# Attention maxima taken one bank at a time, exponentials taken two banks at a time

## The chip, the cores and the metric

The kernel runs on one core of one Trainium2 chip. The metric is the device time of one execution in microseconds (us); the median of three timed runs of the kernel before is 1527.36 us (1527.1 to 1528.5). Of the core's engines this case concerns TensorE (PE, matrix products, and PEld, its weight loads), VectorE (DVE), ScalarE (ACT), GpSimd (POOL) and SyncE (SP, which issues DMAs). TensorE's clock has two levels, 1.2 and 2.4 GHz; a granted clock of 0.50 is the lower one and 1.00 the higher.

## The reference

Two layers follow one another on 4096 tokens of width 128: attention, a mixture of experts, a selective state-space block and a second mixture of experts. Only the attention is touched:

```python
x = L0_attn_x                                   # 4 x 1024 x 128
x = x + _L0_attn_ref(_layernorm(x), wq, w_down, wk_up, wv_up, wo)
...
def _L0_attn_ref(x, wq, w_down, wk_up, wv_up, wo):      # H = 16 heads, D = 8
    q = (x @ wq).reshape(B, T, H, D)
    lat = x @ w_down
    k, v = (lat @ wk_up).reshape(B, T, H, D), (lat @ wv_up).reshape(B, T, H, D)
    q, k = _apply_rope(q, cos, sin), _apply_rope(k, cos, sin)
    scores = jnp.einsum('bqhd,bkhd->bhqk', q, k) * scale
    allowed = pages[None, :] <= pages[:, None]          # pages of 32 tokens
    scores = jnp.where(allowed, scores, finfo.min)
    attn = jax.nn.softmax(scores, axis=-1)
    return jnp.einsum('bhqk,bkhd->bqhd', attn, v).reshape(B, T, E) @ wo
```

## The kernel before

The kernel is a row of blocks, one after another, each with its own instruction list for every engine and semaphores between them. The block concerned is `attend` (from L496). There are 64 pairs of batch and head; they are done in NG = 16 groups of four heads. In a group a "pair" is two heads whose rows lie in partitions 0 to 63 (r = 0) and 64 to 127 (r = 1), so that two matmuls of different r work on different rows of the array.

For every group the work has three strands.

- Maxima. The query-by-key scores are computed once only to find each query's largest score. The allowed blocks of a pair are cut into NK = 9 items of 512 columns, so a group has NI = 18 items. For an item m, `maxima(m)` (L679) writes two PSUM banks, r = 0 and r = 1; `take(m)` (L612) reduces both on VectorE in one instruction over 2 x 512 elements. The item banks are 0 to 3, two per item, so item m needs the banks of item m-2. After the 18th item `combine` (L623) makes the row maxima, GpSimd negates and splits them in bf16 parts, TensorE transposes these (`turn`, L695), ScalarE copies the result to `neg_rows` (`turned`, L644), and SyncE writes them by DMA into rows of the query operand.
- Scores. `scores(i, k, pair)` (L700) computes the key-by-query scores again, now less the maximum, for k = 0 to 8 and two pairs: again two banks of 512 columns. ScalarE exponentiates them, one instruction for each bank (L666), into `prob` in SBUF. The score banks are 4 to 6, used one after another in a ring of three.
- Values. `values(i, v)` (L717) multiplies the values with `prob`, 18 pieces of 256 columns for a group, and accumulates in bank 7. ScalarE copies bank 7 out once a group (`store`, L651).

What sets the order is the loop of the TensorE list (L735 to L756). A lead of LEAD = 26 items of maxima comes first. Then a group has 18 turns, numbered here 0 to 17 (turn = 2k + pair). A turn issues the maxima of one item 26 ahead, the scores of its own k and pair, and the value pieces that are due (L473: one piece in most turns, none in turn 3, two in turn 12). At the end of turn 14 TensorE does the transposition for the next group. All engines take their lists in order, so whatever waits holds up all that stands behind it. The waits around the change are: `maxima(m)` on `max_taken` (L685), `scores` on `exp_done` (L705), in turn 15 also on `neg_stored` (L707), the values of turn 4 on `out_stored` (L726), `take` on `max_scores_done` (L614). ScalarE's `store` of the group before stands between the exponentials of k = 1, pair 1 (L668), and `turned` after the first exponential of k = 7 (L670).

Of the kernel before, what the change touches and what calls it, by code (L numbers as in the profile page):

```python
# [15 lines left out]
P = 128  # L16
# [11 lines left out]
GH = 4  # L28
# [423 lines left out]
]  # L452
NC = 4
MAX_BANK, SCORE_BANK, VALUE_BANK = 0, 4, 7
SCORE_RING = 3
PROB_RING = 4
TURN_K = 7
PIECE = 256
# [37 lines left out]
def attend(nc, g):  # L496

    with ExitStack() as ctx:
# [19 lines left out]
        out_written = [sem(f"out_written{k}") for k in range(2)]  # L518
        block = ctx.enter_context(nc.Block())
        NEG_STEPS = 5  # L520
        UNITS = GH * NK

        def neg_bank(i):

            unit = UNITS * i + GH * TURN_K + 2
            return PS[0:2 * 3 * GP * NJ, SCORE_BANK + unit % SCORE_RING, 0:P // 2].bitcast(BF16)

        def rows(t, count, i, pair, r, first, n):
            return t[HROWS * r:HROWS * r + count, i % RING, pair, first:first + n]

        @block.sync
        def _(sp):
            def store(i):
                sp.wait_ge(out_stored, i + 1)
                sp.dma_start(g.heads[GH * i:GH * (i + 1), :, :, :].rearrange("h k r t -> (h k r) t"), out_sb[:, i % 2, :]).then_inc(out_written[i % 2], 16)

            def neg_in_rows(i):
                sp.wait_ge(neg_stored, i + 1)
                for r in range(2):
                    at, rows_of = HROWS * r + ROWS_QK, 3 * GP * NJ  # L540
                    sp.dma_start(qr[at:at + 3, i % RING, :, :].rearrange("r p t -> r (p t)"),
                                 neg_rows[rows_of * r:rows_of * (r + 1), :]).then_inc(neg_in, 16)

            for n in range(ROWS_BEGUN, RING * ROW_DMAS):
                load_rows(sp, g, n // ROW_DMAS, n % ROW_DMAS)
                if n == 2 * ROW_DMAS - 1:
                    neg_in_rows(0)
            for i in range(NG):
                if i >= 1 and i + RING - 1 < NG:
                    sp.wait_ge(scores_done, UNITS * i)  # L550
                    for n in range(ROW_DMAS):
                        load_rows(sp, g, i + RING - 1, n)
                if i >= 1:
                    store(i - 1)
                if i == NG - 1:

                    for k in range(2):
                        sp.wait_ge(out_written[k], 16 * (EARLY // GH // 2))
                    sp.dma_start(sums[:, :], g.heads[0:EARLY, :, D, :]).then_inc(sums_in, 16)
                    sp.wait_ge(inverted, 1)  # L560
                    sp.dma_start(g.inverses[0:EARLY, :, :].rearrange("i a (k t) -> i (a k) t", k=CPB), sums[:, :]).then_inc(inverse_out, 16)
                else:
                    neg_in_rows(i + 1)
            store(NG - 1)
            for k in range(2):
                sp.wait_ge(out_written[k], 16 * NG // 2)
            sp.wait_ge(inverse_out, 16)
# [39 lines left out]
        @block.vector  # L607
        def _(dve):
            dve.memset(found[:, :, :, :], -3e38).then_inc(bottom_set, 1)
            dve.wait_ge(bottom_set, 1)  # L610

            def take(m):  # L612

                dve.wait_ge(max_scores_done, m + 1)  # L614
                pair, item = divmod(m % NI, NK)
                _, n, first, step = MAXIMA[item]
                bank = MAX_BANK + 2 * (m % 2)
                dve.tensor_reduce(found[:, :, pair, first:first + (n - 1) * step + 1:step],  # L618
                                  PS[:, bank:bank + 2, :].rearrange("p r (w n) -> p r w n", w=n), AX.X, ALU.max).then_inc(max_taken, 1)
                if m % NI == NI - 1:  # L620
                    combine(m // NI)

            def combine(i):  # L623

                dve.wait_ge(max_taken, NI * (i + 1))
                if i > 0:
                    dve.wait_ge(neg_steps, NEG_STEPS * (i - 1) + 1)
                even, odd = (row_max[:, :, :, k::2].rearrange("p r q j -> p (r q) j") for k in range(2))
                every = found[:, :, :, :].rearrange("p r q (j c) -> p (r q) j c", c=NC)
                dve.tensor_reduce(even, every[:, :, 0:NJ // 2, :], AX.X, ALU.max)  # L630
                dve.tensor_reduce(odd, every[:, :, NJ // 2:NJ, :], AX.X, ALU.max).then_inc(row_max_ready, 1)

            for m in range(NG * NI):
                if m % NI == 0 and m > 0:
                    dve.wait_ge(row_max_ready, m // NI)
                take(m)
            dve.wait_ge(sums_in, 16)
            dve.reciprocal(sums[:, :], sums[:, :]).then_inc(inverted, 1)

        @block.scalar  # L640
        def _(act):
            act.preload_act_table(ACT.Exp)

            def turned(i):  # L644

                act.wait_ge(neg_turned, 1 + i + 1)
                if i > 0:
                    act.wait_ge(neg_in, 32 * i)
                act.activation(neg_rows[:, :], neg_bank(max(i - 1, 0)), ACT.Copy).then_inc(neg_stored, 1)

            def store(i):  # L651
                act.wait_ge(values_done, NV * (i + 1))
                if i >= 2:
                    act.wait_ge(out_written[i % 2], 16 * (i // 2))
                act.activation(out_sb[:, i % 2, :], PS[:, VALUE_BANK, :], ACT.Copy).then_inc(out_stored, 1)  # L655

            turned(0)
            for i in range(NG):
                for k in range(NK):
                    step = NK * i + k  # L660
                    if step >= PROB_RING:
                        act.wait_ge(values_done, NV // NK * (step - PROB_RING + 1))
                    for h in range(GH):
                        unit = UNITS * i + GH * k + h
                        act.wait_ge(scores_done, unit + 1)
                        act.activation(prob[:, step % PROB_RING * GH + h, :], PS[:, SCORE_BANK + unit % SCORE_RING, :], ACT.Exp,  # L666
                                       scale=float(D) ** -0.5).then_inc(exp_done, 1)
                        if k == 1 and h == 2 and i > 0:  # L668
                            store(i - 1)
                        if k == TURN_K and h == 0 and i < NG - 1:  # L670
                            turned(i + 1)
            store(NG - 1)

        @block.tensor
        def _(pe):
# [3 lines left out]
            def maxima(m):  # L679

                i, (pair, item) = m // NI, divmod(m % NI, NK)
                if m % NI == 0:
                    pe.wait_ge(rows_in[i % RING], ROW_LOADS * (i // RING + 1))
                if m >= 2:
                    pe.wait_ge(max_taken, m - 1)  # L685
                at = 0
                for q_block, key, n, diagonal in MAXIMA[item][0]:
                    count = ROWS_D if diagonal else ROWS_QK
                    for r in range(2):
                        last = pe.matmul(PS[:, MAX_BANK + 2 * (m % 2) + r, at:at + n], rows(qr, count, i, pair, r, q_block * P, P),  # L690
                                         rows(kr, count, i, pair, r, key, n), start=True, stop=True)
                    at += n
                last.then_inc(max_scores_done, 1)

            def turn(i):  # L695

# [1 line left out]
                pe.transpose(neg_bank(max(i - 1, 0)), neg_parts[:, :, :, :].rearrange("p r s n -> p (r s n)"), g.identb[:, :]).then_inc(neg_turned, 1)  # L698

            def scores(i, k, pair):  # L700
                unit = UNITS * i + GH * k + 2 * pair
                if k == 0 and pair == 0:
                    pe.wait_ge(neg_in, 32 * (i + 1))
                if unit >= 2:
                    pe.wait_ge(exp_done, unit - 1)  # L705
                if k == TURN_K and pair == 1 and i < NG - 1:
                    pe.wait_ge(neg_stored, i + 2)  # L707
                last = {}
                for col, j, q, w, diagonal in KEYS[k]:
                    count = ROWS_D if diagonal else ROWS_M  # L710
                    for r in range(2):
                        last[r] = pe.matmul(PS[:, SCORE_BANK + (unit + r) % SCORE_RING, col:col + w], rows(kr, count, i, pair, r, j * P, P),  # L712
                                            rows(qr, count, i, pair, r, q, w), start=True, stop=True)
                for r in range(2):
                    last[r].then_inc(scores_done, 1)

            def values(i, v):  # L717

                k = v // (NV // NK)
                step = NK * i + k  # L720
                if v % (NV // NK) == 0:
                    pe.wait_ge(exp_done, UNITS * i + GH * (k + 1))
                if v == 0:
                    pe.wait_ge(v1_ready, CPB * (i + 1))
                    if i > 0:
# [13 lines left out]
            for i in range(NG):  # L739
                for k in range(NK):  # L740
                    for pair in range(GP):
# [7 lines left out]
                        for v in DUE[GP * k + pair]:  # L749
                            values(i, v)  # L750
                        if k == TURN_K and pair == 0 and i < NG - 1:
                            pe.wait_ge(exp_done, UNITS * i + GH * TURN_K)
                            turn(i + 1)
            for v in range(NV):
                if due(v) >= 2 * NK:
# [1234 lines left out]
```

## Time and profile before

| | us |
|---|---|
| median of 3 runs | 1527.36 |
| the profiled execution | 1529.38 |
| its span, first to last instruction | 1527.6 |
| VectorE's maxima (L618), first and last start | 93.7 and 441.4 |
| last exponential (L666) starts | 472.2 |

The profile is of one execution. Its span is cut into windows, in which each engine's busy time can be compared with the window's length; the timeline prints single instructions, with runs of equal neighbours merged in one row (start, length of the whole run, engine, line, count). In square brackets stands how long the engine sat idle before, and what ended that. Matmul ends are modelled. On VectorE and ScalarE the record of an instruction overlaps the start of the next one, so the distance from start to start is shorter than the duration of one.

### The profile page before, as it was taken

Reading aid. Unit: us, or ns where it says so; the run is one execution under the profiler, and the core shown is the slowest. Engines: PE = TensorE matmul, PEld = TensorE weight load, DVE = VectorE, ACT = ScalarE, POOL = GpSimd, SP = SyncE. Lnnn points to the kernel's source line nnn. Section 1 sums busy time; section 2 is a strip of 40 time slices with the busy share of each in tenths; the row PEclk is TensorE's granted clock in tenths of the full one; section 3 lists DMA queues with packets and bytes.
Section 4 is the critical chain, followed back from the end, with each engine's and each line's share of the span. In section 5 each row is a group of like instructions: output and inputs, shape, how many; then the busy total and the mean of one; then the engine's idle time right before and its main releaser. Section 6 shows DMA issues by size and latency. Waiting matters only on the chain. (4 is left out here: it accounts for less than half of the span.)

```text
span 1527.6 us, 22335 instructions
## 1 busy us (share of the span) xinstructions
PE 1258.2 (82%) x7696; PEld 582.4 (38%) x7696; DVE 1130.1 (74%) x1298; ACT 720.4 (47%) x1121; POOL 576.3 (38%) x405
## 2 busy tenths in 40 slices
PE   4937999999995769999996676878867867877998
PEld 2412333433333734454443212322322322356565
DVE  5768999999953544444445879999999999964544
ACT  2515999999995133333333783323333323303221
POOL 2320110101002203222334058998989988921000
PEclk9957999999997569999996887998999998985999
DMA  3321111111104200000001004333333323300000
GB/s 101 122 86 48 55 60 45 54 53 59 38 17 113 85 0 0 1 0 0 0 0 28 2 12 145 126 118 107 124 124 124 124 104 108 119 21 9 14 15 27
DMA packets 50302, 91.19 MB, mean 60 GB/s; under 512 B 9495, under 2 KB 25511, under 8 KB 50215
## 3 DMA queue, kind: packets, MB, share of 16 engines
q1 hardware_dynamic: 49710, 89.66, 18.2%
q8 instruction: 54, 0.88, 0.2%
q10 hardware_dynamic: 504, 0.37, 0.1%
q14 instruction: 34, 0.27, 0.1%
HBM read 76.25 MB, written 13.37 MB: 59 GB/s over the span
## 5 line engine op out<-in xcount | busy, mean ns | idle before, releaser
L618 DVE TENSOR_REDUCE att_found<-PS 128x2 f32<-128x1024 f32 (+2 forms) x288 | 333.1, 1218 | 10.8 <-PE PS L690 8.9
L1515 PE MATMUL PS<-ms_ch,ident_sb 128*128 128x512 f32 x512 | 277.6, 670 | 70.3 <-POOL ms_ch L1622 70.3
L666 ACT ACTIVATE att_prob<-PS 128x512 f32<-128x512 f32 x576 | 313.4, 596 | 28.3 <-PE PS L712 15.3
L1622 POOL TENSOR_TENSOR ms_ch<-xnT,ms_c_rows 128x1024 f32<-128x1024 f32 x128 | 302.8, 2378 | 49.2 <-PE PS L1515 26.7
L1580 DVE TENSOR_TENSOR_SCAN xnT<-ms_decay,PS 128x1024 f32<-128x1024 f32 x96 | 216.0, 2275 | 4.5 <-DVE PS L1567 0.5
L731 PE MATMUL PS<-att_prob,att_v 128*32 128x256 f32 (+1 forms) x2560 | 181.8, 370 | 3.0 <-ACT att_out L655 2.8
L1515 PEld LDWEIGHTS PS<-ms_ch,ident_sb 128*128 128x128 f32 x512 | 100.2, 207 | 196.2 <-POOL ms_ch L1622 105.5
L1553 ACT ACTIVATE PS<-m_dt,m_a 128x1024 f32<-128x1024 f32 x32 | 35.8, 1118 | 265.4 <-DVE xnT L1580 265.4
L1027 POOL TENSOR_TENSOR f_yT<-f_yT,f_prod 128x512 f32<-128x512 f32 x56 | 71.0, 1268 | 209.0 <-DVE f_prod L1082 209.0
L690 PE MATMUL PS<-kr,qr 55*128 55x128 bf16 (+4 forms) x1152 | 120.8, 290 | 29.7 <-PEq L256 16.0
L712 PE MATMUL PS<-qr,kr 55*128 55x128 bf16 (+4 forms) x1152 | 114.0, 275 | 14.8 <-ACT att_prob L666 8.2
L1567 DVE TENSOR_TENSOR PS<-ms_dtu,PS 128x1024 f32<-128x1024 f32 x96 | 115.0, 1213 | 12.3 <-PE PS L1506 12.1
L1550 ACT ACTIVATE ms_decay<-m_dt,m_a 128x1024 f32<-128x1024 f32 x96 | 106.2, 1138 | 14.4 <-DVE xnT L1580 14.4
L1082 DVE SCALAR_TENSOR_TENSOR f_prod<-PS,e_w_b,f_x3s 128x512 f32<-128x512 f32 x56 | 42.0, 750 | 84.3 <-PE PS L1151 73.5
L1506 PE MATMUL PS<-m_bc,m_w_sel_b 96*128 96x512 bf16 x192 | 62.9, 413 | 34.9 <-DVE xnT L1580 25.2
L690 PEld LDWEIGHTS PS<-kr,qr 48*128 48x128 bf16 (+1 forms) x1152 | 39.6, 97 | 135.5 <-issue 92.6
L1042 ACT ACTIVATE f_h<-PS,e_w_b 128x512 f32<-128x512 f32 x64 | 44.0, 687 | 94.8 <-PE PS L1139 94.8
L731 PEld LDWEIGHTS PS<-att_prob,att_v 128*32 128x32 f32 x2560 | 54.7, 108 | 62.2 <-issue 53.5
L1629 POOL TENSOR_TENSOR ms_x_row<-ms_dtu,ms_b_row 128x1024 f32<-128x1024 f32 x32 | 75.1, 2346 | 1.3 <-DMA ms_b_row<-bc_rows_dram 1.3
L1580 DVE TENSOR_TENSOR_SCAN xnT<-PS,ms_x_row 128x1024 f32<-128x1024 f32 x32 | 72.5, 2266 | 0.0
L595 POOL COPY att_v<-V 128x256 f32<-128x256 f32 x32 | 11.8, 398 | 156.4 <-PE PS L731 156.1
L177 PE MATMUL PS<-ident_sb,norm_xn 128*128 128x128 f32 x128 | 35.1, 431 | 42.5 <-DVE norm_xn L164 42.0
(214 smaller groups left out, 1784.5 us busy)
## 6 DMA issues: line engine op xcount, KB each, us to landing
ms_c_rows<-bc_rows_dram SPq DMA_DIRECT2D x64, 512.0 KB, 5.6
ms_b_row<-bc_rows_dram SPq DMA_DIRECT2D x32, 512.0 KB, 3.8
qk_parts_dram<-qkv_parts SPq DMA_DIRECT2D x48, 128.0 KB, 1.8
heads_dram<-att_out SPq DMA_DIRECT2D x16, 256.0 KB, 2.4
qr<-qk_parts_dram SPq DMA_DIRECT2D x32, 96.0 KB
qr<-qk_parts_dram SPq DMA_DIRECT2D x96, 32.0 KB
kr<-qk_parts_dram SPq DMA_DIRECT2D x96, 32.0 KB
kr<-qk_parts_dram SPq DMA_DIRECT2D x32, 96.0 KB
```

What stands on the lines that cost most here:

```text
L618: dve.tensor_reduce(found[:, :, pair, first:first + (n - 1) * step + 1:step], PS[:, bank:bank + 2, :].rearrange("p r (w n) -> p r w n", w= ...
L666: act.activation(prob[:, step % PROB_RING * GH + h, :], PS[:, SCORE_BANK + unit % SCORE_RING, :], ACT.Exp, scale=float(D) ** -0.5).then_in ...
L690: last = pe.matmul(PS[:, MAX_BANK + 2 * (m % 2) + r, at:at + n], rows(qr, count, i, pair, r, q_block * P, P), rows(kr, count, i, pair, r, ...
L712: last[r] = pe.matmul(PS[:, SCORE_BANK + (unit + r) % SCORE_RING, col:col + w], rows(kr, count, i, pair, r, j * P, P), rows(qr, count, i, ...
L731: last = pe.matmul(PS[VW * h:VW * (h + 1), VALUE_BANK, q - half * CH:q - half * CH + w], v1[:, i % 2, half, h, j, :], prob[:, step % PROB_ ...
L1027: pool.tensor_tensor(yT[:, k, :], yT[:, k, :], prod[:, e % 2, :], ALU.add).then_inc(summed, 1)
L1515: last = pe.matmul(PS[:, Y_BANK + 2 * half + q, :], g.ident[:, :], ch[:, half, q * CH:(q + 1) * CH], start=j == 0 and not odd, stop=j == J ...
L1550: act.activation(decay[:, 2 * odd + half, :], m.dt[:, half, sequence(b)], ACT.Exp, scale=m.a[:, half, n + odd:n + odd + 1]).then_inc(decay ...
L1567: dve.tensor_tensor(inputs(half), dtu[:, half, :], inputs(half), ALU.mult).then_inc(input_ready, 1)
L1580: dve.tensor_tensor_scan(h[:, odd, half, :], factor, x, 0.0, ALU.mult, ALU.add).then_inc(scanned, 1)
L1622: pool.tensor_tensor(ch[:, half, :], h[:, odd, half, :], c_rows[:, s % C_RING, :], ALU.mult).then_inc(ch_ready, 1)
L1629: pool.tensor_tensor(x_row[:, :], dtu[:, 1, :], b_row[:, :], ALU.mult).then_inc(x_row_ready, 1)
```

## The change

Maxima: the banks become 0 to 2, a ring of three single banks. Each half (r) of an item has its own semaphore count, is reduced by its own VectorE instruction of 512 elements, and frees its own bank. Item m's two banks are those last used by the second half of item m-2 and the first half of item m-1, so TensorE waits for the first half of item m-1. Scores: the banks become 3 to 6, two pairs; one ScalarE instruction of 1024 columns exponentiates both banks of a pair, and `exp_done` and `scores_done` count pairs. `store` now follows the whole exponential of turn 3, and `turned` the whole exponential of turn 14.

```diff
-MAX_BANK, SCORE_BANK, VALUE_BANK = 0, 4, 7
-SCORE_RING = 3
+MAX_BANK, SCORE_BANK, VALUE_BANK = 0, 3, 7
+MAX_RING = 3
...
+        def score_bank(unit):
+            return SCORE_BANK + 2 * (unit % 2)
...
             def take(m):
-                dve.wait_ge(max_scores_done, m + 1)
                 pair, item = divmod(m % NI, NK)
                 _, n, first, step = MAXIMA[item]
-                bank = MAX_BANK + 2 * (m % 2)
-                dve.tensor_reduce(found[:, :, pair, first:first + (n - 1) * step + 1:step],
-                                  PS[:, bank:bank + 2, :].rearrange("p r (w n) -> p r w n", w=n), AX.X, ALU.max).then_inc(max_taken, 1)
+                for r in range(2):
+                    dve.wait_ge(max_scores_done, 2 * m + r + 1)
+                    dve.tensor_reduce(found[:, r, pair, first:first + (n - 1) * step + 1:step],
+                                      PS[:, MAX_BANK + (2 * m + r) % MAX_RING, :].rearrange("p (w n) -> p w n", w=n), AX.X, ALU.max).then_inc(max_taken, 1)
...
-                    for h in range(GH):
-                        unit = UNITS * i + GH * k + h
+                    for pair in range(GP):
+                        unit = PAIR_UNITS * i + GP * k + pair
+                        at = step % PROB_RING * GH + 2 * pair
                         act.wait_ge(scores_done, unit + 1)
-                        act.activation(prob[:, step % PROB_RING * GH + h, :], PS[:, SCORE_BANK + unit % SCORE_RING, :], ACT.Exp,
+                        act.activation(prob[:, at:at + 2, :], PS[:, score_bank(unit):score_bank(unit) + 2, :], ACT.Exp,
                                        scale=float(D) ** -0.5).then_inc(exp_done, 1)
-                        if k == 1 and h == 2 and i > 0:
+                        if k == 1 and pair == 1 and i > 0:
                             store(i - 1)
-                        if k == TURN_K and h == 0 and i < NG - 1:
+                        if k == TURN_K and pair == 0 and i < NG - 1:
                             turned(i + 1)
...
             def maxima(m):
-                if m >= 2:
-                    pe.wait_ge(max_taken, m - 1)
+                if m >= 1:
+                    pe.wait_ge(max_taken, 2 * m + 2 - MAX_RING)
...
-                last.then_inc(max_scores_done, 1)
+                for r in range(2):
+                    last[r].then_inc(max_scores_done, 1)
...
             def scores(i, k, pair):
-                unit = UNITS * i + GH * k + 2 * pair
+                unit = PAIR_UNITS * i + GP * k + pair
                 if unit >= 2:
                     pe.wait_ge(exp_done, unit - 1)
```

On TensorE no instruction moves: the matmuls stand in the same order with waits on the same semaphores, and only the counts and banks differ. On VectorE, at the start of the maxima (`att_found` is where the maxima go, `PS` is PSUM), the list before was:

```order
L618 TENSOR_REDUCE att_found<-PS 128x2 [waits att_max_scores_done,att_bottom_set]
L618 TENSOR_REDUCE att_found<-PS 128x2 [waits att_max_scores_done] x5
L618 TENSOR_REDUCE att_found<-PS 128x2x4 [waits att_max_scores_done]
L618 TENSOR_REDUCE att_found<-PS 128x2x2 [waits att_max_scores_done]
L618 TENSOR_REDUCE att_found<-PS 128x2x4 [waits att_max_scores_done]
L618 TENSOR_REDUCE att_found<-PS 128x2 [waits att_max_scores_done] x6
```

And of the changed kernel, at the same place:

```order
L621 TENSOR_REDUCE att_found<-PS 128x1 [waits att_max_scores_done,att_bottom_set]
L621 TENSOR_REDUCE att_found<-PS 128x1 [waits att_max_scores_done] x11
L621 TENSOR_REDUCE att_found<-PS 128x4 [waits att_max_scores_done] x2
L621 TENSOR_REDUCE att_found<-PS 128x2 [waits att_max_scores_done] x2
L621 TENSOR_REDUCE att_found<-PS 128x4 [waits att_max_scores_done] x2
L621 TENSOR_REDUCE att_found<-PS 128x1 [waits att_max_scores_done] x12
```

Each reduction of two banks has become two of one bank, each with its own wait. On ScalarE, from the first transposed maxima on (`att_neg_rows` is the copy of the transposed maxima, `att_prob` the exponentials, `att_out` the store), the list before was:

```order
L649 ACTIVATE att_neg_rows<-PS 96x128
L666 ACTIVATE att_prob<-PS 128x512 x29
L649 ACTIVATE att_neg_rows<-PS 96x128
L666 ACTIVATE att_prob<-PS 128x512 x14
L655 ACTIVATE att_out<-PS 128x512
L666 ACTIVATE att_prob<-PS 128x512 x22
```

And of the changed kernel:

```order
L652 ACTIVATE att_neg_rows<-PS 96x128
L670 ACTIVATE att_prob<-PS 128x1024 x15
L652 ACTIVATE att_neg_rows<-PS 96x128
L670 ACTIVATE att_prob<-PS 128x1024 x7
L658 ACTIVATE att_out<-PS 128x512
L670 ACTIVATE att_prob<-PS 128x1024 x11
```

The copy stood behind 29 exponentials of 512 columns and stands now behind 15 of 1024, which is one exponential of 512 columns later; the same holds for the store (14 against 7 x 2 after the copy), so both have moved by half a pair.

## Rows read from the trace of the kernel before

**Rows 1.** Windows of the attention: PE, PEld, DVE, ACT, POOL busy, clock, DMA share, GB/s.
```profile
300.00:350.00 50.00, 48.22 (x712) 19.41 (x704) 49.26 (x47) 46.99 (x90) 4.70 (x16) 1.00 0.17 53
...
452.00:475.00 23.00, 18.63 (x264) 6.56 (x261) 3.35 (x1) 20.71 (x39) 0.00 (x0) 1.00 0.10 30
```
**Rows 2.** Durations of single lines (min/median/max ns): maxima, and a 1024-wide ScalarE operation elsewhere.
```profile
L618 DVE TENSOR_REDUCE att_found<-PS x288: 1210/1216/1228, 93.7 to 441.4; 128x2 f32<-128x1024 f32 x96, 128x8 f32<-128x1024 f32 x32, 128x4 f32<-128x1024 f32 x16
...
L1550 ACT ACTIVATE ms_decay<-m_dt,m_a x96: 1132/1134/1151, 917.3 to 1327.2; 128x1024 f32<-128x1024 f32 x96
```
**Rows 3.** Timeline of the lead: start, length, engine, line, operation, count, idle before.
```profile
93.72 20.45 DVE L618 TENSOR_REDUCE att_found<-PS 128x2 f32<-128x1024 f32 x18 [0.63 <-PE PS L690]
...
95.00 0.61 PE L690 MATMUL PS<-kr,qr 48*128 48x512 bf16 x2 [0.96 <-DVE att_found L618]
...
106.31 0.61 PE L690 MATMUL PS<-kr,qr 48*128 48x512 bf16 x2 [0.53 <-DVE att_found L618]
...
114.21 0.22 DVE L630 TENSOR_REDUCE att_row_max<-att_found 128x16 f32<-128x64 f32 x1
...
114.34 0.21 DVE L631 TENSOR_REDUCE att_row_max<-att_found 128x16 f32<-128x64 f32 x1
114.59 10.27 DVE L618 TENSOR_REDUCE att_found<-PS 128x2 f32<-128x1024 f32 x9
...
120.93 0.34 PE L698 MATMUL PS<-identb_sb,att_neg_parts 128*96 128x128 bf16 x1
```
**Rows 4.** Timeline of turns 13 to 16 of one group.
```profile
252.27 0.39 PE L712 MATMUL PS<-qr,kr 55*128 55x128 bf16 x6
...
252.69 1.78 ACT L666 ACTIVATE att_prob<-PS 128x512 f32<-128x512 f32 x3 [0.41 <-PE PS L712]
...
253.16 0.39 PE L690 MATMUL PS<-kr,qr 48*128 48x512 bf16 x2
...
254.28 0.26 PE L698 MATMUL PS<-identb_sb,att_neg_parts 128*96 128x128 bf16 x1
...
254.58 0.27 ACT L649 ACTIVATE att_neg_rows<-PS 96x128 bf16<-96x128 bf16 x1
...
254.97 0.26 PEld L712 LDWEIGHTS PS<-qr,kr 55*128 55x128 bf16 x8 [0.40 <-issue]
...
255.90 0.40 PE L690 MATMUL PS<-kr,qr 55*128 55x128 bf16 x6
...
256.35 13.97 DVE L618 TENSOR_REDUCE att_found<-PS 128x8 f32<-128x1024 f32 x12 [0.21 <-PE PS L690]
```
**Rows 5.** Timeline of the next group's turns 3 to 5, then 11 to 14.
```profile
261.59 0.39 PE L690 MATMUL PS<-kr,qr 48*128 48x512 bf16 x2
...
262.74 0.59 ACT L655 ACTIVATE att_out<-PS 128x512 f32<-128x512 f32 x1
...
263.45 0.19 PEld L731 LDWEIGHTS PS<-att_prob,att_v 128*32 128x32 f32 x8 [0.46 <-issue]
...
264.05 0.39 PE L690 MATMUL PS<-kr,qr 48*128 48x512 bf16 x2
...
270.88 0.39 PE L690 MATMUL PS<-kr,qr 48*128 48x384 bf16 x4
...
272.02 0.39 PE L690 MATMUL PS<-kr,qr 48*128 48x512 bf16 x2
...
273.57 0.39 PE L690 MATMUL PS<-kr,qr 48*128 48x512 bf16 x2
...
275.81 0.26 PE L698 MATMUL PS<-identb_sb,att_neg_parts 128*96 128x128 bf16 x1
```
**Rows 6.** Timeline of the tail, with no maxima left.
```profile
442.25 0.11 PEld L712 LDWEIGHTS PS<-qr,kr 55*128 55x128 bf16 x4 [0.60 <-ACT att_prob L666]
...
456.64 10.45 ACT L666 ACTIVATE att_prob<-PS 128x512 f32<-128x512 f32 x19
...
471.30 0.17 PEld L712 LDWEIGHTS PS<-qr,kr 55*128 55x128 bf16 x6 [0.44 <-ACT att_prob L666]
```

More of the change, by code:

```diff
@@ L520, in attend @@
         NEG_STEPS = 5
-        UNITS = GH * NK
+        PAIR_UNITS = GP * NK
         def neg_bank(i):
-            unit = UNITS * i + GH * TURN_K + 2
-            return PS[0:2 * 3 * GP * NJ, SCORE_BANK + unit % SCORE_RING, 0:P // 2].bitcast(BF16)
+            unit = PAIR_UNITS * i + GP * TURN_K + 1
+            return PS[0:2 * 3 * GP * NJ, score_bank(unit), 0:P // 2].bitcast(BF16)
+        def score_bank(unit):
+            return SCORE_BANK + 2 * (unit % 2)
         def rows(t, count, i, pair, r, first, n):
@@ L549, in _ @@
                 if i >= 1 and i + RING - 1 < NG:
-                    sp.wait_ge(scores_done, UNITS * i)
+                    sp.wait_ge(scores_done, PAIR_UNITS * i)
                     for n in range(ROW_DMAS):
@@ L623, in combine @@
             def combine(i):
-                dve.wait_ge(max_taken, NI * (i + 1))
+                dve.wait_ge(max_taken, 2 * NI * (i + 1))
                 if i > 0:
@@ L683, in maxima @@
                     pe.wait_ge(rows_in[i % RING], ROW_LOADS * (i // RING + 1))
-                if m >= 2:
-                    pe.wait_ge(max_taken, m - 1)
-                at = 0
+                if m >= 1:
+                    pe.wait_ge(max_taken, 2 * m + 2 - MAX_RING)
+                at, last = 0, {}
                 for q_block, key, n, diagonal in MAXIMA[item][0]:
@@ L689, in maxima @@
                     for r in range(2):
-                        last = pe.matmul(PS[:, MAX_BANK + 2 * (m % 2) + r, at:at + n], rows(qr, count, i, pair, r, q_block * P, P),
-                                         rows(kr, count, i, pair, r, key, n), start=True, stop=True)
+                        last[r] = pe.matmul(PS[:, MAX_BANK + (2 * m + r) % MAX_RING, at:at + n], rows(qr, count, i, pair, r, q_block * P, P),
+                                            rows(kr, count, i, pair, r, key, n), start=True, stop=True)
                     at += n
-                last.then_inc(max_scores_done, 1)
+                for r in range(2):
+                    last[r].then_inc(max_scores_done, 1)
             def turn(i):
@@ L707, in scores @@
                     pe.wait_ge(neg_stored, i + 2)
-                last = {}
                 for col, j, q, w, diagonal in KEYS[k]:
@@ L711, in scores @@
                     for r in range(2):
[L712 to L715, printed above, removed]
+                        last = pe.matmul(PS[:, score_bank(unit) + r, col:col + w], rows(kr, count, i, pair, r, j * P, P),
+                                         rows(qr, count, i, pair, r, q, w), start=True, stop=True)
+                last.then_inc(scores_done, 1)
             def values(i, v):
@@ L721, in values @@
                 if v % (NV // NK) == 0:
-                    pe.wait_ge(exp_done, UNITS * i + GH * (k + 1))
+                    pe.wait_ge(exp_done, PAIR_UNITS * i + GP * (k + 1))
                 if v == 0:
@@ L751, in _ @@
                         if k == TURN_K and pair == 0 and i < NG - 1:
-                            pe.wait_ge(exp_done, UNITS * i + GH * TURN_K)
+                            pe.wait_ge(exp_done, PAIR_UNITS * i + GP * TURN_K)
                             turn(i + 1)
```

## The prediction

> **What bounds the kernel now.** I read the windows first, to see which engines are full; then the durations of the lines touched; then the timeline, turn by turn. In a window in the middle of the attention VectorE is busy 49.26 of 50 us, TensorE 48.22 and ScalarE 46.99, at the full clock [rows 1]: three engines near their limits, so the busy shares alone do not decide and the pitches must.
>
> VectorE: one reduction of 1024 elements lasts 1.216 us [rows 2], but in the lead, where it alone is the bound, TensorE is released for items at 95.00 and 106.31, ten items apart, so the pitch is 1.131 us [rows 3]. The pair L630, L631 starts 0.13 us apart for 64 elements each [rows 3]. The two pitches differ by 1.00 us over 960 elements, 1.04 ns each, and leave a fixed part of 0.063 us for an instruction. `combine` puts 0.38 us between two reductions (114.21 to 114.59 [rows 3]). VectorE's need for a group is therefore 18 x 1.13 + 0.38 = 20.7 us.
>
> TensorE: a group takes 21.53 us (the transposition at 254.28, the next at 275.81 [rows 4, 5]), 0.8 more than VectorE needs. An ordinary turn takes 1.14 (270.88 to 272.02; others 1.11 to 1.17, mean about 1.13); turn 12 with its two value pieces 1.55 (to 273.57); turns 3 and 4 together 2.46 (261.59 to 264.05), as turn 3 has no value piece and turn 4 waits for the store [rows 5]; turns 14 and 15 together 2.74 (253.16 to 255.90), with the transposition and the wait for its copy [rows 4]. The sum 13 x 1.13 + 1.55 + 2.46 + 2.74 = 21.4 agrees with 21.53. So TensorE's serial turn bounds a group, VectorE is 4% behind, and two items of buffer let each absorb the other's short stalls.
>
> **The change part by part.**
>
> Reductions. 288 of 1024 elements become 576 of 512. From the line above one costs 0.533 + 0.063 = 0.597, an item 1.193 instead of 1.13. By VectorE alone a group needs 18 x 1.193 + 0.38 = 21.86, above today's 21.53. A half can hardly cost less than its elements, 0.533 (item 1.067), nor more than its full duration, 0.682 (1.216 less 512 elements), item 1.365. These are the ends; I take 0.597, since L630 and L631 show the same fixed part at 64 elements.
>
> On this fixed part the Trainium skill speaks against the change. "VectorE: DVE Perf Modes", in the section on the TRN2 errata, gives a VectorE operation that reads PSUM 120 cycles plus one per element at 0.96 GHz; that is an estimate of 1.192 us for 1024 elements, where the trace has 1.131, and of 0.658 for 512, an item of 1.317. By that rule the sum below would be some 24 us higher. The trace shows about half of the fixed part, so the rule is not what I count with.
>
> The ring of three. Item m now waits for the first half of item m-1. The loop is: first half, 0.682 to its end; 0.06 until TensorE starts (93.72 + 1.216 = 94.94, TensorE at 95.00 [rows 3]); then 0.45 until the reduction starts (255.90 to 256.35 [rows 4]). Sum 1.19: equal to VectorE's own 1.193, with nothing spare. So an ordinary turn takes 1.193 at the high clock, TensorE idling 0.06. More important, nothing is buffered: TensorE can't go ahead in the short turn 3, and each turn of more than 1.19 is idle time of VectorE in full. What stands behind the waiting `maxima` on TensorE are the scores and values of the turn, for which ScalarE waits.
>
> Exponentials. Two of 512 take 2 x 0.547 = 1.094 (19 in 10.45 us, one of them 0.60 long [rows 6]). One of 1024 lasts about 1.134 [rows 2]; less the same overlap of 0.05 its pitch is 1.084. Bounds: 1.067 by the elements, 1.134 by the duration; all below 1.193, so ScalarE is hidden in ordinary turns. With two pairs of banks the scores of turn t wait for exponential t-2, which ends 1.8 us after the start of its turn, against 2.6 when those scores are due: this wait disappears.
>
> The store. It stands after exponential 3. The maxima of turn 3 start at 0; the scores follow at 0.23 and the exponential 0.42 behind them (252.27 to 252.69 [rows 4]), so at 0.65; the store at 0.65 + 1.08 = 1.73; the values of turn 4 start 0.71 after the store does (262.74 to 263.45 [rows 5]), at 2.44, and the next turn 0.57 to 0.60 later, at 3.02. Without the wait it would be 2.39. Before it was 2.46: +0.56 a group.
>
> The copy. Turn 14's maxima at 0, exponential at 0.65, transposition at 1.12 as before (253.16 to 254.28), but the copy only after the whole exponential, at 1.73 instead of 1.42. The scores of turn 15 start 0.39 after the copy does (254.58 to 254.97 [rows 4]), at 2.12, and turn 16 0.9 later, at 3.02 against 2.74: +0.28. Those 0.39 and 0.71 may vary by 0.1.
>
> Combine: 0.38 on VectorE was hidden behind TensorE's longer group; now TensorE waits for it: +0.38. Turn 12 stays at 1.55.
>
> A group: 13 x 1.193 + 0.38 + 1.55 + 3.02 + 3.02 = 23.48 against 21.53, +1.95. The maxima run beside 262 turns. Groups 1 to 13 are complete: 13 x 1.95 = 25.4. Of group 0 some turns run at the low clock, with TensorE bound as before; I count 9 turns x 0.06 + 0.38 + 0.28 = 1.2. Of group 14 ten turns have maxima: 8 x 0.06 + 0.56 = 1.0. Together 27.6 us.
>
> The lead, 26 items at the low clock. A matmul of 512 columns lasts 0.61 instead of 0.39 [rows 3, 4], so the loop is 0.682 + 0.06 + 0.67 = 1.41 an item, more than VectorE's 1.193. The first transposition stands behind item 24. It was at 120.93; it will be at 94.47 (item 1) + 23 x 1.41 + 0.16 (combine, as far as it outlasts the loop) + 0.54 = 127.6: +6.7. If the latencies overlapped entirely it would be 24 x 0.063 = 1.5.
>
> The tail, 26 turns without maxima, bound by ScalarE: from 442.25 to 471.30, 25 turns in 29.05 us [rows 6]. Now 25 x 1.084 + 0.48 (store) + 0.17 (copy) + 0.64 (ScalarE idle from the copy until the scores of turn 15) = 28.4: -0.7, between -1.5 and +1.
>
> Sum: 27.6 + 6.7 - 0.7 = +33.6. The span 1527.6 becomes 1561.2, the profiled execution (1.8 more) 1563.0; the median lay 2.0 below the profiled execution, so 1561.
>
> **The rivals.**
>
> 1. The loop between the engines is a little longer than 1.19, by 0.05 (the second wait, or a half finished later by the other's matmul). For: the sum has no slack. Against: all its parts are measured. Price 0.05 x 13 x 14.5 = 9 us: 1571.
>
> 2. Only VectorE's extra time counts; the stalls of turns 4, 12 and 15 are absorbed and the lead runs at VectorE's pitch. For: TensorE is idle 0.06 a turn. Against: that is all that it could make up. Price: (21.86 - 21.53) x 14.5 + 1.5 - 0.7 = +5.6: 1533.
>
> 3. A half is paced by its full duration, 0.682, an item 1.365: 13 x 0.172 x 14.5 = 32 more, 1594. For: the next half stands behind a wait of its own. Against: every reduction today stands behind a wait too and has a pitch 0.085 under its duration [rows 2, 3]. The Trainium skill's rule belongs here ("VectorE: DVE Perf Modes", on the DRAIN that can't be avoided: the next operation does not start until the pipe is empty); by the durations of this trace that rule would give this rival's time, and the 1.131 against 1.216 contradicts it.
>
> 4. Not slower. The fixed part is hidden for a single bank (half at 0.565 or below), so VectorE stays behind TensorE, and the two pairs of score banks take away TensorE's waits for ScalarE: turns 14 and 15 fall to 2.44, turns 3 and 4 to 2.26. Price -0.5 x 14.5 = -7: 1520. It decides from an item below 1.13 and a store that is not later. Against: the fixed part at 64 elements, and the move of both ScalarE copies.
>
> 5. The clock falls where TensorE idles more. Against: in the tail it was busy only 18.63 of 23 us at clock 1.00 [rows 1], and it will be busy nearly 90%. With half the turns at the low clock, three matmul stages each 0.22 longer: 130 x 0.6 = 78 more, 1640.
>
> **How the numbers follow.** Forecast 0.62, rival 1 0.14, rival 2 0.12, rival 3 0.06, rival 4 0.04, rival 5 0.02. The predicted time is the forecast's, 1561, its own range 1550 to 1570 (0.02 us on each of 13 x 14.5 turns is 4 us; 0.1 on both ScalarE releases is 3; 3 for the lead). For 8 in 10 I take in rival 1 and the space toward rival 2, in which part of the stalls would be absorbed: 1543 to 1576. A measurement can tell about 0.2% from no change. Slower: forecast and rivals 1, 2, 3 and 5, 0.96; of rival 4, faster 0.03 and same 0.01.
>
> **What would show it.** In the changed profile: reductions of 0.68 us at a pitch of 0.60; a group from transposition to transposition 23.5 us; in the lead 1.41 an item, with VectorE idle 0.2 before every first half; TensorE's values of turn 4 released by the store and its scores of turn 15 by the copy, with VectorE idle about 0.6 after each; ScalarE no longer the releaser of scores in ordinary turns; clock 1.00 throughout. The forecast is wrong if a group takes under 22.5 us (the stalls are absorbed) or over 24.5 (the pitch or the loop is longer).

## The result and the profile after

The changed kernel takes 1555.46 us, median of 4 runs (1554.67 to 1555.91); the kernel before, timed beside it, 1527.23 (1526.43 to 1528.5). The ratio is 1.0184, with a 95% interval of 1.0166 to 1.0201: 28.2 us slower. The forecast was 1561, own range 1550 to 1570. The profiled execution took 1555.27 us, its span is 1553.5.

The timeline of the lead, in the columns of [rows 3]; L621 are the reductions, L694 the maxima's matmuls, L633 the first instruction of `combine`, L703 the transposition:

```profile
93.64 24.93 DVE L621 TENSOR_REDUCE att_found<-PS 128x1 f32<-128x512 f32 x36 [0.61 <-PE PS L694]
...
95.78 0.61 PE L694 MATMUL PS<-kr,qr 48*128 48x512 bf16 x2 [0.78 <-DVE att_found L621]
...
109.69 0.61 PE L694 MATMUL PS<-kr,qr 48*128 48x512 bf16 x2 [0.78 <-DVE att_found L621]
...
127.23 0.34 PE L703 MATMUL PS<-identb_sb,att_neg_parts 128*96 128x128 bf16 x1
```

From 95.78 to 109.69 there are ten items, 1.39 us each, where [rows 3] has 1.13. The first transposition is at 127.23 instead of 120.93: the lead costs 6.3 us.

The durations (min/median/max ns), against [rows 2]:

```profile
L621 DVE TENSOR_REDUCE att_found<-PS x576: 677/679/693, 93.6 to 473.2; 128x1 f32<-128x512 f32 x128, 128x4 f32<-128x512 f32 x32, 128x2 f32<-128x512 f32 x32
...
L670 ACT ACTIVATE att_prob<-PS x288: 1018/1023/1072, 131.5 to 500.6; 128x1024 f32<-128x1024 f32 x144
```

A reduction of 512 lasts 0.679, an exponential of 1024 lasts 1.023.

One group in the timeline, from transposition to transposition; the same places as [rows 4, 5]:

```profile
269.43 0.26 PE L703 MATMUL PS<-identb_sb,att_neg_parts 128*96 128x128 bf16 x1
...
277.23 0.39 PE L694 MATMUL PS<-kr,qr 48*128 48x512 bf16 x2
...
278.80 0.59 ACT L658 ACTIVATE att_out<-PS 128x512 f32<-128x512 f32 x1
...
279.54 0.64 PE L734 MATMUL PS<-att_prob,att_v 128*32 128x256 f32 x8 [0.50 <-ACT att_out L658]
280.11 0.39 PE L694 MATMUL PS<-kr,qr 48*128 48x512 bf16 x2
...
280.53 6.07 DVE L621 TENSOR_REDUCE att_found<-PS 128x1 f32<-128x512 f32 x10 [0.37 <-PE PS L694]
...
291.69 0.39 PE L694 MATMUL PS<-kr,qr 48*128 48x512 bf16 x2
...
292.81 0.26 PE L703 MATMUL PS<-identb_sb,att_neg_parts 128*96 128x128 bf16 x1
...
293.33 0.27 ACT L652 ACTIVATE att_neg_rows<-PS 96x128 bf16<-96x128 bf16 x1
...
293.74 0.41 PE L716 MATMUL PS<-qr,kr 55*128 55x128 bf16 x8 [0.35 <-ACT att_neg_rows L652]
...
294.65 0.40 PE L694 MATMUL PS<-kr,qr 55*128 55x128 bf16 x6
...
295.08 5.47 DVE L621 TENSOR_REDUCE att_found<-PS 128x4 f32<-128x512 f32 x9 [0.37 <-PE PS L694]
```

The group is 292.81 - 269.43 = 23.38 us, against 21.53. Turns 3 and 4 (277.23 to 280.11) take 2.88: the values stand until the store lets go of bank 7. Turns 14 and 15 (291.69 to 294.65) take 2.96: the scores stand until the copy is through. After each, VectorE is idle (the brackets of its two rows). VectorE's waits come just behind TensorE's: with no spare bank the stall is handed on.

The busy time in the window of [rows 1]:

```profile
300.00:350.00 50.00, 44.54 (x640) 17.05 (x642) 47.62 (x82) 40.66 (x44) 4.70 (x16) 1.00 0.16 50
```

All three engines are less busy than before, at the full clock. ScalarE has less to do (one exponential of 1.023 us where there were two of 0.597), but TensorE has the same matmuls and VectorE a little more than before, so neither is full: what sets the pace is a loop of waits. Who waited for whom says the same (us in total, times, longest; 150 to 440 us). First of the kernel before:

```profile
PEld PS L690 <- DVE att_found L618: 14.5, 40, 0.4
PEld PS L712 <- ACT att_prob L666: 12.1, 29, 0.6
...
DVE att_found L618 <- PE PS L690: 4.5, 14, 1.7
```

Then of the changed one:

```profile
PEld PS L694 <- DVE att_found L621: 89.4, 173, 1.1
ACT att_prob L670 <- PE PS L716: 49.1, 150, 0.8
...
DVE att_found L621 <- PE PS L694: 13.0, 39, 0.7
```

Where the time went: +6.3 to the first transposition; +24.1 from there to the last (447.79 became 478.18, by its line's first and last start); -1.6 in the rest of the attention, whose last store starts at 502.82 instead of 474.02. That is +28.8 for the attention, near the medians' +28.2. The two profiled spans differ by 25.9 only; the difference shrinks by 3 us in the state-space stage, which did not change, and the kernel before alone varied by more than that between executions. I do not assign them.

### The profile page after: what moved, and what is told of

It reads as the page before. It is cut to its first block and busy times, and to the rows that moved or that the text cites. A ratio compares the mean times of both kernels' runs of the same rounds, so it can differ in the third digit from the quotient of the medians.

```text
span 1553.5 us, 22335 instructions
## 1 busy us (share of the span) xinstructions
PE 1258.4 (81%) x7696; PEld 576.9 (37%) x7696; DVE 1151.0 (74%) x1586; ACT 700.0 (45%) x833; POOL 577.4 (37%) x405
## 5 line engine op out<-in xcount | busy, mean ns | idle before, releaser
L621 DVE TENSOR_REDUCE att_found<-PS 128x1 f32<-128x512 f32 (+2 forms) x576 | 354.0, 681 | 21.1 <-PE PS L694 17.6
L1518 PE MATMUL PS<-ms_ch,ident_sb 128*128 128x512 f32 x512 | 269.5, 652 | 72.1 <-POOL ms_ch L1625 72.1
L670 ACT ACTIVATE att_prob<-PS 128x1024 f32<-128x1024 f32 x288 | 293.0, 1024 | 72.8 <-PE PS L716 65.1
L694 PE MATMUL PS<-kr,qr 55*128 55x128 bf16 (+4 forms) x1152 | 121.0, 290 | 54.2 <-DVE att_found L621 35.8
L694 PEld LDWEIGHTS PS<-kr,qr 48*128 48x128 bf16 (+1 forms) x1152 | 39.6, 96 | 176.5 <-DVE att_found L621 138.8
```

The source lines that it names most:

```text
L621: dve.tensor_reduce(found[:, r, pair, first:first + (n - 1) * step + 1:step], PS[:, MAX_BANK + (2 * m + r) % MAX_RING, :].rearrange("p (w ...
L670: act.activation(prob[:, at:at + 2, :], PS[:, score_bank(unit):score_bank(unit) + 2, :], ACT.Exp, scale=float(D) ** -0.5).then_inc(exp_don ...
L694: last[r] = pe.matmul(PS[:, MAX_BANK + (2 * m + r) % MAX_RING, at:at + n], rows(qr, count, i, pair, r, q_block * P, P), rows(kr, count, i, ...
L1518: last = pe.matmul(PS[:, Y_BANK + 2 * half + q, :], g.ident[:, :], ch[:, half, q * CH:(q + 1) * CH], start=j == 0 and not odd, stop=j == J ...
```

## The experiments

Theory A is that of the prediction: a loop through both engines without a spare bank, VectorE's fixed part twice, and ScalarE releases moved half a pair later. Rival B: the number of VectorE instructions is all of it. Rival C: the wide exponentials and their late releases are most of it. Each ratio is to the kernel before on the same chip, with its 95% interval (it is not the quotient of the two medians beside it, and differs from that by up to 0.0013); a "group" is the distance of two transpositions near 250 to 300 us.

| run | us | before beside it | ratio | group, us |
|---|---|---|---|---|
| before | | | 1 | 21.53 |
| changed | 1555.5 | 1527.2 | 1.0184 (1.0166 to 1.0201) | 23.38 |
| e1, ring of three, narrow scores | 1546.9 | 1528.1 | 1.0128 (1.0101 to 1.0154) | 22.73 |
| e2, split, four banks | 1534.3 | 1528.1 | 1.0041 (1.0026 to 1.0056) | 22.05 |
| e3, store early | 1546.5 | 1528.1 | 1.0109 (1.0088 to 1.0129) | 22.91 |
| e4, store and copy early | 1542.5 | 1529.3 | 1.0084 (1.0057 to 1.0110) | 22.71 |
| e5, a wait for each half | 1550.3 | 1528.1 | 1.0142 (1.0123 to 1.0160) | 23.35 |
| e6, e4 and e5 | 1539.9 | 1529.3 | 1.0057 (1.0016 to 1.0098) | 22.69 |
| e7, half of each reduction | 1527.8 | 1529.3 | 0.9991 (0.9973 to 1.0010) | 21.93 |
| e9, before, even pieces | 1525.0 | 1529.3 | 0.9967 (0.9948 to 0.9986) | 21.24 |
| e10, e9 and e11 | 1520.6 | 1528.7 | 0.9958 (0.9944 to 0.9972) | 21.24 |
| e11, before, DMA first | 1525.5 | 1528.7 | 0.9982 (0.9973 to 0.9991) | 21.53 |

**e1 and e2: the parts of the maxima.** Both are the kernel before with split reductions; e1 has the ring of three, e2 keeps four banks:

```diff
+MAX_RING = 3        # e1; e2: MAX_RING = 4
-                if m >= 2:
-                    pe.wait_ge(max_taken, m - 1)
+                if m >= 1:          # e2: if m >= 2
+                    pe.wait_ge(max_taken, 2 * m + 2 - MAX_RING)
```

> The maxima as changed (three single banks, two reductions an item), the scores and exponentials as before (three single banks, 512 wide). Theory A (a loop without a spare buffer, plus late ScalarE releases): the lead costs what it does in the changed kernel, 6.3 us, at 1.39 us an item. A group is 13 ordinary turns of 1.19, 0.4 for combine, 1.55 for turn 12, 2.5 for turns 3 and 4 (store after a narrow exponential) and 2.74 for turns 14 and 15, 22.7 us: about +22 us, 1549. Theory B (only the number of VectorE instructions counts): a group of 21.9 and +7 to +9 in all, 1535. Theory C (the wide exponentials and their late releases are most of it): below +10, under 1537.

> The kernel before with each reduction split in two of 512, but with four maxima banks, so that TensorE may be a whole item ahead. Theory A: only VectorE's fixed part shows, 0.063 an item: lead +1.6 at 1.19 an item, a group 18 x 1.19 + 0.38 = 21.9 against 21.5, together +6.5 us, 1534. Theory B says that this is all of the change: +28, 1555. If VectorE's extra instruction cost nothing it would be 1527.

e2 is +6.2 us, as theory A had it, and B falls: the same 576 reductions cost a fifth of the change. Its timeline shows VectorE full:

```profile
254.94 21.63 DVE L619 TENSOR_REDUCE att_found<-PS 128x1 f32<-128x512 f32 x36
```

That is (21.63 - 0.68) / 35 = 0.599 us from start to start. e1 is +18.8: the same instructions, one bank fewer, 12.6 us more. C falls as the main cause, since two thirds of the loss are there without any wide exponential. From before to e2 to e1 to the changed kernel the group grows by 0.52, 0.68 and 0.65 us: fixed part, missing bank, late releases, about a third each.

VectorE's own starts in one such group say where. In e2 they are 0.599 apart except around `combine`, which adds 0.49. In e1 three waits of VectorE come on top: 0.23 behind turns 14 and 15, 0.32 behind turn 12 with its two value pieces, 0.08 behind the transposition; these the fourth bank absorbed. In the changed kernel they are 0.45, 0.32 and 0.08, and 0.45 more behind the store. Together that is 1.30 us on e2's 22.05, and the changed kernel's group is 23.38.

**e3 and e4: the releases.**

```diff
-                        if k == 1 and pair == 1 and i > 0:     # behind the exponential
-                            store(i - 1)
+                        if k == 1 and pair == 1 and i > 0:     # ahead of it (e3, e4)
+                            store(i - 1)
...
+                        if k == TURN_K and pair == 0 and i < NG - 1:          # e4
+                            act.activation(prob[:, at, :], PS[:, score_bank(unit), :], ...)
+                            turned(i + 1)
+                            act.activation(prob[:, at + 1, :], PS[:, score_bank(unit) + 1, :], ...)
+                            (wait for both halves, then count exp_done up by one)
```

> The changed kernel with the store of bank 7 ahead of the exponential of turn 3 instead of behind it. Theory A: turns 3 and 4 fall from 2.88 to 2.39 us, 14 times: -6.9 us against the changed kernel, 1548.5. If that stall were hidden by something else (the maxima's loop being the bound there too), no change, 1555.

> The changed kernel with the store ahead of the exponential of turn 3, and the exponential of turn 14 split in two of 512 with the copy of the transposed maxima between them. Theory A: on top of the early store (1546.5 measured) turns 14 and 15 fall from 2.96 to about 2.66 us, -0.3 x 14.5 = -4: 1542. If the two late releases were all of the loss (theory C) this kernel would be at 1531 or below, since then only lead and pitch are left.

The group falls by 0.47 and then 0.20, 0.67 in all, which is what the wide exponentials had added (0.65). e3's gain of 9 us, by the medians of two different chips, is larger than the expected 6.9. By the traces the attention's last store starts 7.1 us earlier (495.74 against 502.82), and 2.0 of these come from the tail, which has the store too: from the last transposition to the last exponential it takes 20.4 us (473.1 to 493.5), in the changed kernel 22.4 (478.2 to 500.6).

**e5 and e6: loosening the loop.**

```diff
-                if m >= 1:
-                    pe.wait_ge(max_taken, 2 * m + 2 - MAX_RING)
...
+                for r in range(2):
+                    if 2 * m + r >= MAX_RING:
+                        pe.wait_ge(max_taken, 2 * m + r + 1 - MAX_RING)
+                    (all pieces of half r)
+                    last.then_inc(max_scores_done, 1)
```

> The changed kernel, but TensorE does all pieces of the first half of an item and then all of the second, each behind its own wait: the first half needs only the second half of item m-2, so it can be written while VectorE still reduces the first half of item m-1. Theory A: the lead falls from 1.39 to 1.19 us an item (-4.9); in the groups VectorE has half an item of buffer, 21.9 to 22.4 us against 23.4: together -19 to -26, 1530 to 1536. If the separate order costs TensorE the overlap of its two row halves (0.1 to 0.2 us in the six items of several pieces), up to 1542. Theory B (instructions only): 1555, no change.

> Both early releases and the separate wait for each half together. The separate wait alone gave the lead back (-4.3 us) but nothing in the groups, 23.5 us each. Theory D (revised: in the groups TensorE's own turns are the bound as soon as the loop is loosened, and its waits for ScalarE are in them): now that those waits are short the group is 22.0 to 22.5, in all 1530 to 1537. If the maxima's ring alone still set the pace, the group would stay at 22.7 or more and the time above 1538.

Here I missed. The lead shrank, by 3.9 us where I expected 4.9: the first transposition came at 123.31, and VectorE's first twelve halves take 7.26 us, 0.598 apart. But e5's group stayed at 23.35, and e6's at 22.69 is no better than e4's 22.71. The timeline of TensorE in e6 has ordinary turns of 1.20 us:

```profile
276.34 0.43 PE L700 MATMUL PS<-kr,qr 55*128 55x128 bf16 x5
...
277.54 0.42 PE L700 MATMUL PS<-kr,qr 48*128 48x128 bf16 x7
...
278.75 0.41 PE L700 MATMUL PS<-kr,qr 55*128 55x128 bf16 x5
...
279.94 0.41 PE L700 MATMUL PS<-kr,qr 48*128 48x384 bf16 x3
```

These rows show no wait, but the timeline prints idle time only from about 0.15 us on, and the waits here are shorter. VectorE runs through all of this without a pause (first row below, 0.598 from start to start), and the weights of the second half are loaded just when one of its reductions ends (second and third row, from narrow windows):

```profile
266.12 14.44 DVE L622 TENSOR_REDUCE att_found<-PS 128x4 f32<-128x512 f32 x24
...
274.50 0.68 DVE L622 TENSOR_REDUCE att_found<-PS 128x1 f32<-128x512 f32 x1
...
275.23 0.09 PEld L700 LDWEIGHTS PS<-kr,qr 48*128 48x128 bf16 x1
```

The reduction ends at 275.18, the load starts 0.05 later. The longer waits alone, in the columns of the list above for the whole of 150 to 440 us, are many:

```profile
PEld PS L700 <- DVE att_found L622: 36.9, 87, 0.8
```

In a steady group of e6 the second half starts 0.05 us after the end of a reduction in each of the turns 0 to 12. So 1.20 is VectorE's pitch for two halves, and TensorE waits for it in every such turn. Where it does not, the separate order costs it next to nothing: turn 16 takes 1.14 in e6 and 1.13 in the kernel before.

The edit explains why. The changed kernel waits for `max_taken` to reach 2m + 2 - 3 = 2m - 1. In e5 and e6 the second half (r = 1) waits for 2m + 1 + 1 - 3, which is the same count. Only the first half's matmuls have moved ahead of that wait; the rest of the turn, with the scores for ScalarE, stands behind it as before. In the lead a turn is nothing but the two halves, so there the early half shortens the loop. In the groups VectorE's waits are those of e4, 0.23, 0.32 and 0.08 us. The half item of buffer that I counted on does nothing for the groups, and theory D's first half (TensorE is the bound once the loop is loose) is not tested by e6.

**e7: half of VectorE's work.** It leaves out part of the computation: the maxima are over half of the columns.

```diff
-                                      PS[:, MAX_BANK + (2 * m + r) % MAX_RING, :].rearrange(...)
+                                      PS[:, MAX_BANK + (2 * m + r) % MAX_RING, 0:BANK // 2].rearrange(...)
```

> The changed kernel, but each reduction reads only the first 256 of its 512 columns (the maxima are then of half the keys; everything after runs as before). VectorE needs 13 us a group and the loop through it shrinks by 0.27 us. Theory D: ordinary turns fall to TensorE's own 1.13, the late releases stay: 13 x 1.13 + 1.55 + 2.88 + 2.96 = 22.1 a group, -19 in all, and the lead falls to 1.13 an item, -6.5: 1530, no faster than the kernel before although VectorE does half. If VectorE's pitch and combine were all of the loss, a group would be under 21.5 and the time under 1521.

The timeline around turns 3 to 6 and 14 to 16 of TensorE:

```profile
262.83 0.39 PE L694 MATMUL PS<-kr,qr 48*128 48x512 bf16 x2
...
265.14 0.64 PE L734 MATMUL PS<-att_prob,att_v 128*32 128x256 f32 x8 [0.79 <-ACT att_out L658]
265.71 0.39 PE L694 MATMUL PS<-kr,qr 48*128 48x512 bf16 x2
...
266.82 0.39 PE L694 MATMUL PS<-kr,qr 48*128 48x512 bf16 x2
...
276.19 0.39 PE L694 MATMUL PS<-kr,qr 48*128 48x512 bf16 x2
...
279.15 0.40 PE L694 MATMUL PS<-kr,qr 55*128 55x128 bf16 x6
```

Ordinary turns are down to 1.11, while turns 3 and 4 are still 2.88 and turns 14 and 15 still 2.96. With VectorE at 31.55 of 50 us the kernel is no faster than the one before. This is the run that shows theory D: with VectorE out of the way TensorE's own turns are the bound, and the stalls that ScalarE causes are TensorE's, independent of VectorE.

**e9, e11, e10: a version faster than both.** What bounds the kernel before is TensorE's own list, so the next kernel changes that: one value piece in every turn, none empty and none doubled. And the DMA of the negated maxima, for which TensorE waited 1.6 us once behind 36 row loads on SyncE's queue, goes ahead of the last eight of them.

```diff
 def due(v):
-    return v + 4 if v < NV // 2 else v + 3
+    return v + 4                                  # e9, e10
...
-            for n in range(ROWS_BEGUN, RING * ROW_DMAS):
+            for n in range(ROWS_BEGUN, RING * ROW_DMAS - 8):       # e10, e11
...
                     neg_in_rows(i + 1)
+                    for n in range(RING * ROW_DMAS - 8, RING * ROW_DMAS) if i == 0 else ():
+                        load_rows(sp, g, n // ROW_DMAS, n % ROW_DMAS)
```

> The kernel before, with value piece v always due four turns on: one piece in every turn, none empty and none doubled (turn 3 has the last piece of the group before, turn 12 one instead of two). TensorE bounds this kernel, so what counts are its waits: turns 3, 4 and 12 took 0.61 + 1.85 + 1.55 = 4.0; now 1.13 + 1.13 + 1.13 and a wait for the store of about 0.4: 3.8, -0.2 a group, -3 in all, 1525. If the store now holds the values of turn 4 for longer (0.8), 0 to +3.

> The kernel before with the same move of the 8 row loads alone. Its trace has a wait of 1.6 us for that DMA, once, which the changed kernel doesn't have, as its groups are longer. Theory E: -1.5 us, ratio 0.999, at the edge of what can be told; the profile has to show the wait gone. That would also be 1.6 us that the changed kernel gave back.

> The kernel before with value pieces always four turns on, and the last 8 row loads of group 3 issued after the DMA of group 1's negated maxima instead of ahead of it. In the run with even pieces TensorE waited 3.0 us once, at the first turn of group 1, for that DMA, which stood behind the row loads. Theory E: that wait goes and VectorE's stall with it: 2 to 3 us on top of the even pieces' 4.3, together -6 to -7 against the kernel before, ratio 0.996 to 0.995. If the wait is only passed on to another, no more than the even pieces alone, 0.997.

The wait in the kernel before, and in e9 (waits of 150 to 190 us; waited for, total, times, longest):

```profile
PE PS L712 <- DMA qr<-att_neg_rows: 1.6, 1, 1.6
```

```profile
PE PS L712 <- DMA qr<-att_neg_rows: 3.0, 1, 3.0
```

In e10 and e11 no such row is left. e10 is 0.42% faster than before (0.28 to 0.56%), 6.4 us by its ratio, and 2.2% under the changed kernel. Even pieces give 0.29 us a group, where I expected 0.2.

This wait stands in every kernel of the table but e10 and e11, and it is not the same in all: 0.4 us in the changed kernel, 1.3 to 3.0 in the others. What it costs shows in the second group, from the second transposition to the third, against a steady group: 1.7 us more in the kernel before, 0.4 in the changed one, 3.1 in e2, 3.0 in e5, 4.3 in e6, 5.9 in e9. So the totals of these runs differ by some us for a reason that is none of the theories', and the group is the safer measure. In e9 it took back most of the gain: the last transposition of its trace is only 0.4 us earlier than before (447.42 against 447.79). What even pieces are worth is read from e10 against e11, 441.98 against 445.75: 3.8 us.

## Why the prediction was right

The forecast was 5.5 us above the result, in its own range. By its steps:

- Reductions: a half at 0.597, an item at 1.193. e2 measured 0.599. The Trainium skill ("VectorE: DVE Perf Modes", the section on the TRN2 errata) gives 120 cycles plus one per element at 0.96 GHz, an estimate of 0.658 for this instruction; that differs from the measurement, and the measurement decides. The same page's section on the DRAIN that can't be avoided says that the next operation waits for an empty pipe; taken so, as the prediction took it, the trace contradicts it: 0.679 long, 0.599 apart. But the section goes on to say that a next operation that is not held starts earlier, and this the prediction left out. Rivals 3 and 4 fall with that.
- The ring of three, a loop of 1.19 with nothing spare: ordinary turns are 1.17 to 1.20, and e1 against e2 shows the missing bank as a cost of its own, 12.6 us. Rival 2, in which the stalls are absorbed, would have been e2; rival 1, a longer loop, was not seen.
- The lead, +6.7: measured +6.3 at 1.39 an item instead of 1.41.
- The copy, turns 14 and 15 at 3.02: measured 2.96. The store, turns 3 and 4 at 3.02: measured 2.88.
- `combine`, 0.38: measured 0.49 on VectorE in e2, as it also has to wait for the end of the last reduction (0.71 from that reduction's start instead of 0.60).
- The group, 23.48: measured 23.38. The closeness is in part luck, as `combine` came out 0.11 too small and the two stalls 0.20 too large. The clock stayed at 1.00 (300 to 350 us); rival 5 was not seen.

The forecast for the attention was +33.6, and the trace has +28.8; three mis-sized terms make up most of the difference. First, the exponential of 1024. I took 1.134 from a ScalarE row whose input is not in PSUM and whose scale is read from memory for each partition, where the exponential here has a constant one; which of the two makes it longer, no run shows. I even called 1.067 the lower bound, which was VectorE's rate. The exponential lasts 1.023, and in the tail seven of them take 6.63 us, 0.935 apart:

```profile
479.56 6.63 ACT L670 ACTIVATE att_prob<-PS 128x1024 f32<-128x1024 f32 x7 [0.59 <-PE PS L716]
```

That made the store's stall 0.14 smaller in each group, and the tail shorter: -1.6 from the last transposition to the last store, just outside the -1.5 to +1 that I gave. The Trainium skill ("VectorE: DVE Perf Modes", the section on the TRN2 errata) has a figure for ScalarE too, 172 cycles plus one per element at 1.2 GHz from PSUM; that is an estimate of 0.997 us, and the trace, at 1.023, agrees with it to 3%, better than the row that I chose. Second, the kernel before had a single wait of 1.6 us for a DMA that stood behind row loads, and in the changed kernel it is 0.4, which makes 1.3 us in the second group. Why it is short there is open: e3 reaches its second transposition within 0.3 us of the changed kernel and waits 1.5. e11 showed that this wait is real time (ratio 0.9982). It was in the trace and I had not looked for single long waits. Third, the turns at both ends of the attention, where I had counted by whole groups: from the first transposition to the next the change costs 0.9 us where I had 1.2, and around the last group 0.3 where I had 1.0.

## What to carry to other kernels

A ring in which the producer writes two slots and the consumer frees one at a time has to be measured as a loop: time to free one, hand over, refill both, hand back. If that equals the consumer's own pitch, every irregular step of the producer is lost in full. To loosen such a loop, look at the count that the last wait of a turn is for: moving work ahead of a wait leaves the loop as it is when what the next engine needs still stands behind the same count (e5). And a wait that is too short for the timeline to print can still set the pace: compare the start of an instruction with the end of what it needs. And when instructions are merged to save a fixed part, ask what stood between the merged halves: here a store and a copy, each the release of another engine, moved half a pair back and cost as much as the missing bank.

## What was unexpected of the hardware

VectorE's fixed part is nearly the same for a reduction of 64 elements from SBUF and for one of 512 or 1024 from PSUM: with 1.04 ns an element, 0.066 to 0.069 us between starts (0.136, 0.599 and 1.131 us apart). ScalarE passes 1024 elements from PSUM to SBUF in 1.023 us and 512 in 0.597, 0.83 ns an element, where the row with its input elsewhere and its scale from memory took 1.134 for 1024. A TensorE weight load that waits for a VectorE reduction starts 0.05 us after the reduction's end, again and again in e5 and e6. And the order of the matmuls of two row halves hardly matters in these turns: issued half after half a turn with three pieces to a half takes 1.14 us, alternating 1.13 (turn 16 of e6 and of the kernel before).
